# A two-layer mixture-of-experts kernel: bank-by-bank borders of the first experts, and the first layer's gate from exponential, addition and reciprocal, with its joins and products on GpSimd

## The reference

```
xn = layernorm(x)
s  = attention(xn)            # causal, 16 heads of 8, softmax, times WO
g  = silu(experts(xn))        # 8 experts, top 2 of 8, silu(x w1) * (x w3), w2
x  = x + s * g
xn = layernorm(x)
s  = recurrent block(xn)      # phases, prefix sums, layernorm, gelu MLP
g  = silu(experts with capacity(xn))
x  = x + s * g
```

## Time and profile before

| what | us |
|---|---|
| three runs | 614.62, 616.67, 618.25; median 616.67 |
| the profiled execution, its own time | 616.33 |
| its span, first to last instruction | 614.5 |
| TensorE busy | 573.1 (93%) |
| VectorE busy | 476.7 (78%) |
| ScalarE busy | 330.9 (54%) |
| GpSimd busy | 190.4 (31%) |
| mean granted TensorE clock | 0.981 of full speed |

### The profile page before, as it was taken

How to read it: one execution, slowest core, us unless ns; L and a number is a source line. 1 busy time by engine, 2 the same in 40 slices (tenths; PEclk the granted TensorE clock), 3 DMA queues, 4 the chain that set the end, 5 groups by cost and what they waited for, 6 DMA issues and landing times.

```text
span 614.5 us, 11961 instructions
## 1 busy us (share of the span) xinstructions
PE 573.1 (93%) x3901; PEld 352.2 (57%) x3902; DVE 476.7 (78%) x1307; ACT 330.9 (54%) x602; POOL 190.4 (31%) x221
## 2 busy tenths in 40 slices
PE   2878999999999999899999998989899999999996
PEld 1433544444444534899999963535446665656554
DVE  6799889999989898455555578666899899976465
ACT  2762567676777776555555558864223642362224
POOL 1451000000254452133333310000007685688300
PEclk9898899999999999999999999999999999999999
DMA  8955727070813171211111034215011322421412
GB/s 185 210 182 206 241 77 216 3 217 1 224 31 109 53 226 20 56 49 47 47 47 47 26 97 128 71 41 151 0 46 25 97 59 54 130 79 40 126 42 68
DMA packets 55612, 57.99 MB, mean 94 GB/s; under 512 B 8651, under 2 KB 39403, under 8 KB 55515
## 3 DMA queue, kind: packets, MB, share of 16 engines
q1 hardware_dynamic: 51242, 50.56, 29.9%
q0 software_dynamic: 4320, 6.81, 3.5%
HBM read 41.96 MB, written 18.85 MB: 99 GB/s over the span
## 4 chain that ended last, share of the span: by engine, by line
PE 76%; DVE 16%; ACT 4%; issue 2%; DMA 1%; SPq 1%; ACTq 0%; DVEq 0%
PE banks L1689 11%; PE banks L1831 10%; PE banks L1756 8%; PE banks L1778 7%; PE banks L1964 7%; PE banks L1701 6%; PE banks L1953 5%; PE banks L1950 5%; PE banks L2015 4%; DVE banks L1239 4%; DVE mpart L1242 3%; PE banks L1759 2%; ACT arena L809 1%; PE banks L1840 1%; PE banks L1598 1%
## 5 line engine op out<-in xcount | busy, mean ns | idle before, releaser
L809 ACT ACTIVATE arena<-banks 128x512 f32<-128x512 f32 (+1 forms) x304 | 154.3, 583 | 75.1 <-PE banks L1759 40.7
L1239 DVE CUSTOM_DVE_ANT_0 banks<-banks,arena 128x512 f32<-128x512 f32 (+3 forms) x256 | 119.7, 511 | 9.2 <-PE banks L1778 8.3
L1756 PE MATMUL banks<-arena 128*128 128x512 bf16 (+3 forms) x384 | 116.6, 331 | 4.0 <-ACT arena L809 2.8
L1778 PE MATMUL banks<-arena 96*128 96x512 bf16 (+3 forms) x384 | 113.5, 336 | 4.8 <-DVE mpart L1239 2.7
L1242 DVE TENSOR_REDUCE mpart<-banks 128x1 f32<-128x512 f32 x128 | 85.8, 683 | 9.1 <-PE banks L1778 8.1
L1689 PE MATMUL banks<-arena 128*128 128x128 f32 x624 | 76.3, 275 | 1.0 <-ACT arena L743 1.0
L1689 PEld LDWEIGHTS banks<-arena 128*128 128x128 f32 x624 | 72.8, 192 | 1.5 <-ACT arena L743 1.5
L1831 PE MATMUL banks<-arena 128*9 128x512 f32 (+3 forms) x768 | 70.7, 487 | 0.0
L851 ACT ACTIVATE arena<-banks 125x512 f32<-125x512 f32 (+2 forms) x48 | 28.4, 595 | 71.2 <-PE banks L1950 46.2
L1756 PEld LDWEIGHTS banks<-arena 128*128 128x128 bf16 x384 | 37.8, 99 | 49.6 <-issue 23.8
L620 POOL DMA_INDIRECT results<-arena x39 | 37.7, 967 | 77.4 <-DVE arena L1133 77.4
(11 more groups left out here) (295 smaller groups left out, 858.0 us busy)
## 6 DMA issues: line engine op xcount, KB each, us to landing
k_parts<-arena SPq DMA_DIRECT2D x6, 768.0 KB, 8.1
arena<-in_L_ffn_experts_w_dram SPq DMA_DIRECT2D x2, 2048.0 KB, 11.1
arena<-results SPq DMA_DIRECT2D x8, 512.0 KB, 6.6
arena<-k_parts SPq DMA_DIRECT2D x7, 576.0 KB
arena<-q_parts SPq DMA_DIRECT2D x28, 144.0 KB
arena<-in_L_ffn_w_kernel_dram SPq DMA_DIRECT2D x8, 344.0 KB, 3.8
slots<-in_pad_rows_dram SPq DMA_DIRECT2D x1, 2535.0 KB, 12.3
arena<-slots SPq DMA_DIRECT2D x39, 65.0 KB, 1.8
```

What stands on the lines that cost most here:

```text
L809: act.activation(Pr[:, r % 4, heads[0]:heads[-1] + 1, 0:n], ring_e[e % 3][:, 0:len(heads) * n].rearrange("p (j c) -> p j c", j=len(heads)) ...
L1239: ins = dve.tensor_tensor_reduce(unmasked, unmasked, tail_mask[:, 512 - n:512], 1.0, -BIG, ALU.add, ALU.max, part[:, at:at + 1])
L1756: ins = pe.matmul(ring_e[e % 3][:, at * n:at * n + n], QK[:, slot, j, 1, P * kt:P * kt + P], QK[:, slot, j, 0, q:q + n], start=True, stop= ...
L1778: ins = pe.matmul(ps[:, at * n:at * n + n], QK[0:TALL, slot, j, 0, P * i:P * i + P], QK[0:TALL, slot, j, 1, 512 * half:512 * half + n], st ...
```

## The change

It has three parts.

1. At the entry, block 0's weights are gathered in a new step `first_weights`, one stage ahead of the experts (behind `turn` (5, 1), at stage 2), with the waits that go with it; the first eight blocks are loaded right behind the mrow DMA of (6, 0), ahead of that of (6, 1); ScalarE begins with a Silu of two columns.
2. At the exit, the last block's down product goes to bank 6 and becomes the step `last_rows`, behind the first exp step after the experts, with its own store. The bank of every unit comes from a table: the bank unused longest, and, behind the experts, each bank with its own event (`AFTER_EXPERTS`). TensorE no longer waits for the last result.
3. The gate: `combine` runs on GpSimd; ScalarE computes exp(-y) instead of Silu; GpSimd adds 1; VectorE takes the reciprocal; y * s is GpSimd's for the first half (`product`), y * reciprocal is VectorE's in `finish` for the first half and GpSimd's (`gate1`) for the second.

```diff
-          16: [("combine", 0)], 19: [("combine", 1)], 21: [("gate", 0), ("gate", 1)], 25: [("finish", 0)], 26: [("finish", 1)],
-          28: [("norm", 0)], 30: [("norm", 1)], 39: [("x_turn", 0)], 41: [("x_turn", 1)], 45: [("logits1",)], ...
+          16: [("combine", 0)], 19: [("combine", 1)], 21: [("gate", 0), ("one_more", 0), ("product",)], 22: [("gate", 1)], 24: [("inverse", 0)], 25: [("finish", 0)], 26: [("finish", 1)],
+          28: [("norm", 0)], 30: [("norm", 1)], 32: [("one_more", 1)], 36: [("inverse", 1), ("gate1",)], 39: [("x_turn", 0)], 41: [("x_turn", 1)], 45: [("logits1",)], ...
...
+E_BANKS, M_BANKS = (0, 1, 2), (3, 4, 5, 6)
+AFTER_EXPERTS = ((2, ("sg_done", NB0 - 1)), (0, ("sg_done", NB0)), (1, ("hid_done", NB0)),
+                 (3, ("hid_done", NB0 - 1)), (4, ("a_sb", NB0)), (5, ("y_done", NB0 - 1)), (6, ("y_done", NB0)))
...
+    def take(banks, n, freed):
+        bank = min(banks, key=lambda i: (used[i], i))
+        before, used[bank], held[bank] = held[bank], n, freed
+        return bank, before
...
+            if step[0] == "experts0":
+                for order, (bank, freed) in enumerate(AFTER_EXPERTS):
+                    used[bank], held[bank] = n + order / 10, freed
...
 # SyncE, for g == EXPERTS_AT[0] + 1
                     sp.dma_start(iota, bass.AP(pos_rows.tensor, 2 * S, [[0, P], [1, C1]])).then_inc(Z["ld_iota"], 16)
-                    first_blocks()
                     later_blocks()
...
-                    if (g, half) == (EXPERTS_AT[0] + 1, 0):
+                    if (g, half) == (EXPERTS_AT[0], 0):
+                        first_blocks()
+                    elif (g, half) == (EXPERTS_AT[0] + 1, 0):
                         load_results()
...
-            sp.wait_ge(Z["f_done"], 2)
+            sp.wait_ge(Z["gate1_in"], 1)
             sp.dma_start(pscale, ...)
...
 # GpSimd
+                    elif step[0] == "combine":
+                        pool.wait_ge(ld_y[step[1]], 32)
+                        pool.tensor_tensor(ya[:, tiles, :], ya[:, tiles, :], yb[:, tiles, :], ALU.add).then_inc(Z["f_done"], 1)
+                    elif step[0] == "one_more":
+                        pool.wait_ge(Z["gated"], step[1] + 1)
+                        pool.tensor_scalar(yb[:, tiles, :], yb[:, tiles, :], 1.0, None, ALU.add).then_inc(Z["one_more"], 1)
+                    elif step[0] == "product":
+                        pool.wait_ge(Z["out_in"], 2)
+                        pool.tensor_tensor(ya[:, 0:8, :], ya[:, 0:8, :], s_sb[:, 0:8, :], ALU.mult).then_inc(Z["product_in"], 1)
+                    elif step[0] == "gate1":
+                        pool.wait_ge(Z["inverted"], 2)
+                        pool.tensor_tensor(ya[:, 8:16, :], ya[:, 8:16, :], yb[:, 8:16, :], ALU.mult).then_inc(Z["gate1_in"], 1)
...
 # ScalarE
             def experts0():
-                act.wait_ge(Z["ld_moe0"], 48)
-                act.wait_ge(Z["blkpos_ready"], 1)
-                gather_w3(0, 0)
+                act.activation(sg0[:, 0, 0:2], C[:, C_ID:C_ID + 2], ACT.Silu)
                 x_copy(0, 0)
...
                     elif step[0] == "gate":
-                        gate_half(0, step[1])
+                        act.wait_ge(Z["f_done"], step[1] + 1)
+                        act.activation(yb[:, tiles, :], ya[:, tiles, :], ACT.Exp, scale=-1.0).then_inc(Z["gated"], 1)
...
 # VectorE
+            def first_weights():
                 dve.wait_ge(Z["ld_moe0"], 48)
                 dve.wait_ge(Z["e_ready"], EXP_UNITS * EXPERTS_AT[0])
                 dve.wait_ge(Z["blkpos_ready"], 1)
                 gather_w1(0, 0)
...
+            def last_rows():
+                result(NB0 - 1, NB0 - 1, (NB0 - 1) // YB0, mixed_last)
...
+                if layer == 0:
+                    dve.wait_ge(Z["inverted"], 1)
+                    dve.wait_ge(Z["product_in"], 1)
+                    link(dve.tensor_tensor(ya[:, tiles, :], ya[:, tiles, :], yb[:, tiles, :], ALU.mult))
...
-                    elif step[0] == "combine":
-                        combine(ld_y[step[1]], 32, step[1])
+                    elif step[0] == "inverse":
+                        dve.wait_ge(Z["one_more"], step[1] + 1)
+                        dve.reciprocal(yb[:, tiles, :], yb[:, tiles, :]).then_inc(Z["inverted"], 1)
...
 # TensorE
-                if not isinstance(j, int) or j >= 1:
+                if not isinstance(j, int) or 1 <= j < NB0 - 1:
                     pe.wait_ge(Z["y_done"], j)
...
-                down(NB0 - 1, NB0 - 1)
...
-                if unit >= 4:
-                    name, n = FREES[unit - 4]
+                if M_AFTER[unit] is not None:
+                    name, n = M_AFTER[unit]
                     pe.wait_ge(Z[name], n)
-                return ring_m[unit % 4]
+                return banks[:, M_BANK[unit], :]
...
                         experts0()
-                        pe.wait_ge(Z["y_done"], NB0)
+                    elif step[0] == "last_rows":
+                        down(NB0 - 1, NB0 - 1, mixed_last)
```

More of the change, by code:

```diff
@@ L222, in ring_tables @@
             if step[0] == "maxrow":
                 frees.append(("mrow_ready", 2 * step[1] + step[2] + 1))
-            elif step[0] in RING_STEPS:
+            else:
                 reads += 1
                 frees.append(("m_free", reads))
[L227 to L232, removed]
+            bank, before = take(m_banks, n, frees[-1])
@@ new lines, in ring_tables @@
+            m_bank.append(bank)
+            m_after.append(before)
+        elif step[0] in ("negmax", "experts0"):
+            reads_before[step] = reads
+            if step[0] == "experts0":
+                for order, (bank, freed) in enumerate(AFTER_EXPERTS):
+                    used[bank], held[bank] = n + order / 10, freed
+    return frees, unit_of, reads_before, reads, e_bank, e_after, m_bank, m_after
+FREES, UNIT_OF, READS_BEFORE, READS, E_BANK, E_AFTER, M_BANK, M_AFTER = ring_tables()
@@ L358, in build @@
         psO = banks[:, 6:8, :].rearrange("p a c -> p (a c)")
-        ring_e = [banks[:, i, :] for i in range(3)]
-        ring_m = [banks[:, 3 + i, :] for i in range(4)]
         O = banks[:, 7, :]
-        turned_in, mixed = banks[:, 4, 0:P], banks[:, 5, 0:D]
+        turned_in, mixed, mixed_last = banks[:, 4, 0:P], banks[:, 5, 0:D], banks[:, 6, 0:D]
         names = """sum_ps sum_sb ld_const bc_done rows_in half_ready sqrt0_in sqrt0_out ld_spread stacked_done sel_ps sel_a sel_d ld_proj ld_moe0 ld_posr ld_L1 pads_in pads1_in xn_ready xT_ps xT_sb proj_ps
@@ L800, in _ @@
                             act.wait_ge(mrow_in[half], 16 * (g - 1))
-                        act.copy(mrow[0:3 * HG, g % 2, 512 * half:512 * half + 512], ring_m[unit % 4][0:3 * HG, :]).then_inc(Z["mrow_ready"], 1)
+                        act.copy(mrow[0:3 * HG, g % 2, 512 * half:512 * half + 512], banks[0:3 * HG, M_BANK[unit], :]).then_inc(Z["mrow_ready"], 1)
                     elif step[0] == "exp":
```

72 lines of the change are left out of this document (49 added, 23 removed).

## The result

The changed kernel takes 630.89 us (median of four runs, 630.17 to 633.33), the kernel before, timed again beside it, 615.77 (614.62 to 618.25). The ratio of the two, over all runs, is **1.0226** with a 95% interval of [1.0185, 1.0267], which is 14 us slower; the medians are 15.1 us apart. The profiled execution took 631.51 us, its span is 629.7 and the mean granted clock 0.964, against 616.33, 614.5 and 0.981. The forecast of 626.4 had the sign and the mechanism, and was 4.5 us short.

A forecast was written before the change was run, and what follows sets the result against it. TensorE bounds the kernel nearly everywhere, but at the gate VectorE's queue is as long. Two reciprocals make the logits +8.1 us late, the low clock adds 1.6: +9.7, 626.4 us on the median, range 621.0 to 632.0.

The forecast's parts named there:

- The reciprocal: Gate on VectorE: two reciprocals of 128x1024 at 6.55 us each, both in VectorE's chain ahead of the logits.
- Its start: Gate: VectorE through its maxima reads, so the first reciprocal starts, at 377.5, TensorE arriving about 2.4 us earlier.
- the borders: Entry to and exit from the experts: 2.0 us gained together, arriving at the gate.
- Entry: Start of the experts: 0.27 us gained at the first transpose and 0.27 at the gap behind it, together 0.5.
- Exit: End of the experts: TensorE goes on without waiting, VectorE's second maxima read at 358.65 instead of 360.18, 1.5 us gained.
- The clock: Behind TensorE's second pause the granted clock may fall: 1.6 us for one spell, bounds 0 and 3.2.
- one_more: GpSimd's addition of 1 in the gate: taken at 2.3 us, allowed from 1.0, eight short ones would be 6.9.
- rival 2: Gate on GpSimd: one_more takes 6.9 us, the first reciprocal starts 3.8 later, 630.2 us; chance 0.12.
- rival 1: Gate on VectorE: long reciprocals cost what a tensor_tensor costs, 1.22 us, giving 614.1 us, faster by 0.4%; chance 0.12.
- rival 3: Gate on VectorE: a long reciprocal takes eight steps a column, 8.7 us, giving 630.7 us; chance 0.06.
- rival 4: Behind the logits, 395 to 413: TensorE's 2.27 us idle closes and the clock holds, giving 622.5 us; chance 0.15.
- rival 5: Entry and exit of the experts: a bank comes free late, nothing of the 2.0 us arrives, 628.4 us; chance 0.08.

The follow-up runs named there:

- experiment 5: Changed kernel with the second reciprocal and gate1 moved behind the route's places: ratio 1.0178 to the kernel before.
- experiment 6: Changed kernel with the first reciprocal moved behind the last maxima read and its reduction: ratio 1.0213 to the kernel before.
- experiment 3: Changed kernel with both reciprocals replaced by a tensor_tensor subtraction of the same tile: ratio 1.0016 to the kernel before.
- experiment 4: Changed kernel with silu by tanh, one GpSimd instruction with two constants and no reciprocal: ratio 0.9959 to the kernel before.
- experiment 9: Changed kernel with tanh gate, block 0's w1 gathered inside the experts behind VectorE's last maxima read: ratio 0.9937 to the kernel before, later 0.9944.
- experiment 1: New entry and exit with the old gate of the kernel before: ratio 0.9963 to the kernel before.
- experiment 10: Old gate with new entry and exit, block 0's w1 gathered inside the experts: ratio 0.9983 to the kernel before.
- experiment 11: Tanh gate with old entry and exit: ratio 0.9976 to the kernel before; with new ones and w1 gathered inside the experts, beside it: 0.9944.
- experiment 8: Changed kernel with sixteen idle TensorE products in the pause ahead of the logits: ratio 1.0147 to the kernel before.
- experiment 7: Changed kernel with GpSimd's addition of 1 written as times 1 plus 1: 626.63 us in one execution, kernel before 615.58.

## Why the prediction was right, and where it was short

**The reciprocal** was right: 6.55 us twice, and the sum along VectorE's queue with it. The second decimal is luck: the trace's own 51 ns for eight more columns, not rounded to 6.25 a column, would have given 6.68. From the end of the first reciprocal (385.44) to the end of the copies (404.64) are 19.20 us; the prediction had 12.59 and 6.55, 19.14. Both pauses are where it put them, 7.05 and 4.60 us long, where it had 6.9 and 5.7. Experiments 5 and 6 say that it is the sum of the queue more than a place in it; experiments 3 and 4, that it is the reciprocal.

**Its start** was 1.4 us late: 378.89 instead of 377.5. That is mostly a mis-sized term of the sum, the borders. The prediction let 2.0 us of them, and 0.41, arrive at the gate: the last maxima product ahead of the reciprocal was to end at 376.7. It ended at 377.73, 1.4 us earlier than before (379.13) instead of 2.4. VectorE's reads ended 1.06 us behind it instead of 0.8, at 378.79, and one_more at 378.85, hardly later. The chain to the logits became +9.7 instead of +8.1.

- **Entry**, "together 0.5": the change at the first transpose was a loss of 0.3 (3.10 against 2.77), and between the first two blocks' products the gap shrank as forecast (250.61 less 248.10 is 2.51, before 2.84). Nothing is left. The step that failed is "so 246.1 becomes 246.56": it counted the copy, at 0.46 (0.43 measured), and left out the 0.53 of issue in front of it. TensorE now starts 0.10 behind VectorE's last maxima read (247.34, in experiment 9 246.45), so what stands ahead of that read is paid.
- **Exit**, "1.5 gained": right at the first unit, not at the gate. VectorE's read of the second pair is at 358.55, before 360.18, as forecast:

```profile
357.23 0.69 DVE L1294 TENSOR_REDUCE mpart<-banks 128x1 f32<-128x512 f32 x1
358.12 0.35 DVE L1174 TENSOR_SCALAR arena<-banks,arena 128x128 f32<-128x128 f32 x1 [0.20 <-PE banks L1761]
358.39 0.15 DVE L1175 COPY arena<-arena 128x1 int32<-128x1 int32 x1
358.55 0.70 DVE L1291 CUSTOM_DVE_ANT_0 banks<-banks,arena 128x512 f32<-128x512 f32 x1
```

  TensorE kept a lead of 1.6 us over the kernel before up to 366.04 (there 367.65). At 369.35 (there 370.06) it was 0.7. VectorE lost its part first, in an idle of 0.56 us ahead of its reads at 365.28, which the kernel before doesn't have; TensorE then waits 0.35 at L1897. Why VectorE stood idle there stays open. In whole runs the borders brought 0.2 to 0.4% (1 to 2.3 us, experiments 1, 10 and 11, and not clear of noise in the last two), so 2.0 was at the upper end.

**The clock** was the larger error: +1.6 for one spell, bounds 0 and 3.2, measured 5.5, outside the bounds. The prediction took one spell with the cost of one in the kernel before; in the changed kernel it lasted 10.2 us instead of 3.4 behind the second pause (3.4 us lost by the time it ended: TensorE's turn of the last heads is at 425.04, before at 411.90, so the lag had grown from 9.7 to 13.1), and the one at the phases grew too (another 2.1). The prediction took its price from the phases' row, and left the phases themselves at no change. Together, 1.6 us in the chain and 3.9 in the clock are the 5.5 by which the profiled spans (15.2 apart) exceed the sum of +9.7; the medians' 4.5 is less because the forecast stood on 616.67. Experiment 8 shows that the pause has a part in the low clock behind it. How long a spell gets is not explained: the executions of experiments 6 and 7 had shorter ones behind the same pause.

**one_more** cost 2.78 us, between the bounds, nearer to "an add with a second input" than to eight short ones; rival 2 (6.9 us) did not come, and since it ended together with VectorE's reads it cost next to nothing by itself (experiment 7). By the Trainium skill, "GPSIMD Engine Reference", section "3.1 Elementwise — side-by-side cycle accounting", the prediction's estimate was 1.5 us: the form with one operation took nearly twice that, the form with two less, 1.04.

**The rivals.** 1 (a long reciprocal at 1.22 us) was the only way to a gain, and is out by the row of 6.55; experiment 3, which puts a tensor_tensor there, gave 1.0016, though its first one took 3.40 us, so a price of 1.22 each was not tried. 3 is out by the same row: 8 steps of 1.04 ns would be 8.7 us. The Trainium skill, "VectorE: DVE Perf Modes", section "First, the fixed hardware budget", states a repeat count of 8 for Reciprocal; read as 8 cycles a column, as the prediction did for its estimate, it would be 8.7 us, and the trace disagrees with that reading. 4, part won back, went the other way: behind the logits 5.5 us were lost. 5 is out: of the borders' 2.0 us and the 0.41, 1.4 arrived at the gate.

## What to carry to other kernels

Price a long instruction by the slope of two short ones of its kind: 202 ns at 8 columns and 253 at 16 gave 6.55 us at 1024 (6.68 without rounding), and 6.55 was measured. Where the queue that the others wait for is full, moving an added instruction brings little back (1.0178 and 1.0213 against 1.0226 here); what would have to go is the instruction, here by an identity (silu by tanh) whose table is the one already loaded. And price a pause of TensorE with the low clock that follows it: here about a third of a microsecond for each at 1.2 GHz, over spells of 6.8 or 10.2 us behind a pause of 4.0 to 4.7.

## What the runs showed of the hardware that was not expected

- GpSimd's tensor_scalar on 128x1024 float32 took 2.78 us with one operation (add 1) and 1.04 with two (times 1, plus 1), both times in each run.
- ScalarE took Tanh between exponentials without a table load; the old gate's Silus had one of 1.28 us on either side.
- VectorE's tensor_tensor on 128x1024 took 3.40 us beside GpSimd's tensor_tensor and 1.22 alone; the reciprocal took 6.55 either way.
- Behind a pause of 4.60 us the granted clock was at 1.2 GHz for 10.2 us, in other executions with a pause of 4.0 to 4.7 us there for 6.8. Filled with idle products up to its last microsecond, the pause was followed by 3.4 us, and the kernel was 0.8% faster than the changed one.
- VectorE's reciprocal takes 6.4 ns a column at 1024 columns, where the tensor_tensor has 1.2.
